# AdaLN layers on one core: setup cut to two modulation rows, step sizes finished per batch and stored in rows, half of the recurrence's first block loaded ahead

## The chip, the cores and the metric

The kernel runs on one core of a Trainium2 chip. The metric is the device time of one execution in microseconds (us); lower is better. All compute engines of the core take part: TensorE (PE in the profile, with PEld for its weight loads), VectorE (DVE), ScalarE (ACT), GpSimd (POOL). SyncE (SP) issues every DMA, from one queue.

## The reference

Two layers work on 16 batches of 512 tokens of 256 channels. Each layer has an attention part and a feed-forward part, each of them with a shift, a scale and a gate that come from a small conditioning vector per batch:

```python
mod = silu(c) @ wmod                       # per layer: 6 vectors of 256 for each batch
h = layernorm(x) * (1 + scale) + shift
# layer 0, attention part: a test-time-trained memory
q, k = l2norm(silu(short_conv(h @ W)));  v = silu(short_conv(h @ Wv))
lr = softplus(h @ Wlr.T + 0.001)           # two step sizes per token and head
# for each chunk of 16 tokens, one after the other:
k_h = softmax(k W_in) * lr[..., 1:];  q_h = softmax(q W_in)
o = q_h W_out + causal(q_h k_h) v
W_in, W_out = updated twice with lr of the chunk's first token
# then: o = layernorm(o) * gate @ Wo, a low-rank FFN, window attention, a gated FFN
```

The gates of both layers pass through a rule that keeps their size at 0.25 or more, with their sign.

## The kernel before, in words

Everything is one program, with semaphores set by hand: each engine has its own list of steps, and the order of the code is the order of execution. `Steps` names the values of a semaphore; `wait_ge(x.sem, x.at(n, "name"))` waits until that step of round n is done.

- **Setup.** SP loads the conditioning vectors and both layers' `wmod` (2 x 1.5 MB), three constants and 24 weights (`weights_loaded`). PE makes all 24 column blocks of the modulation (96 matmuls in the trace, L719) and the four gate rows (16, L725). ACT copies them out of PSUM, DVE adds one to the scales and makes the gates' sign and size in four dependent operations (L1749 to L1755). SP stores them in `gates_d`, and only behind this store, in the same queue, stands the first load of `x` (L488).
- **Phase A**, one iteration for each of 16 batches, on all engines at once. DVE: statistics of the next batch (L1762), for six tiles a convolution of three operations (L1785), and squares for the norms of q and k (L1794). ACT: `Ln` of the norms (L1223), the first step of the next layer norm (L1179, L1182), then for each tile the first tap of the convolution (L1201), between them `Exp` (L1187, L1227); then rows of k (L1236), `silu` of the tiles (L1211), gates (L1216), the raw step sizes (L1255) and the modulation of the next batch (L1194). PE: projections (L763), transposes (L736, L779), means of squares (L799). POOL: q and k times their inverse length (L1534). SP: stores of q and k (L492), the load of the next x but one (L488), `v_rows` and `k_rows` (L514), v, the gate, and the raw step sizes in `lr_d` (L514). `x` has one buffer (`a_x`).
- **`phase_a_done`**: every engine waits until all stores of phase A have landed, since the memory (`arena`) is used again with another layout.
- **Set-up of the recurrence.** SP loads the step sizes (L550, four DMAs in pieces of 64 bytes), twelve pieces of the first block of q, k, v (L557) and eight of the first chunk's rows (L565). ACT makes `Abs`, `Exp` and `Ln` of the 128 x 2048 step sizes, DVE adds the positive part (L1839) and copies every second one; PE picks rows (L820); POOL and DVE set areas to zero; POOL's last area, `kv`, stands in the memory in which the step sizes lie, so it waits for PE and DVE.
- **Recurrence** over 32 chunks, from PE's first sums (L846), then the other layers, two batches at a time, to the end.

The softplus is written as max(x, 0) + ln(1 + exp(-|x|)).

Of the kernel before, what the change touches and what calls it, by code (L numbers as in the profile page):

```python
# [6 lines left out]
P = 128  # L7
BATCH, TOK, DIM = 16, 512, 256
HEADS, HD = 16, 16
KT = DIM // P  # L10
# [62 lines left out]
def adaln_two_layers(nc, x, w_in, taps, w_out, ln_g, ln_b, w_in_init, w_out_init, u1, v1, b1, u2, v2, b2,  # L73
                     cond, wmod, w_attn, w_proj, w_r, w_k, w_v, mu, ident_c, blocks_c, parity_c, mask_c, four_c, scan_c, out):
    ctx = ExitStack()
    with ctx:
# [16 lines left out]
        lr_d = dram("lr_d", [CHUNKS, BATCH, CHUNK, 2 * HEADS])  # L93
# [43 lines left out]

        wmod_sb = carve(LAYERS, KT, N_MOD * DIM)
        cond_sb = carve(LAYERS, KT, BATCH)
        cond_silu = carve(LAYERS, KT, BATCH)  # L140
        g_raw = carve(2 * LAYERS * DIM)
        g_sign = carve(2 * LAYERS * DIM)
        g_size = carve(2 * LAYERS * DIM)
        gates_row = arena[0:BATCH, ARENA - 2 * LAYERS * DIM:ARENA]
# [18 lines left out]
        a_rows = [carve(TT, 2 * TOKROW) for _ in range(2)]  # L163

# [10 lines left out]
        kq_blk = [carve(TILES * 2 * BLOCK).rearrange("p (j g s t) -> p j g s t", j=JJ, g=GG, s=2) for _ in range(2)]  # L175
        v_blk = [carve(TILES * BLOCK).rearrange("p (j g t) -> p j g t", j=JJ, g=GG) for _ in range(2)]
        o_blk = [carve(TILES, BLOCK) for _ in range(2)]
        k_rows, v_rows = ([carve(TILES, ROW17) for _ in range(2)] for _ in range(2))
        kv = carve(JJ, PP * INNER * HD)
        run = carve(JJ, PP * INNER * HD)  # L180
# [15 lines left out]
        lr_raw, lr_tmp = (t.rearrange("p a b -> p (a b)") for t in (kv, run))  # L196
# [64 lines left out]
        su_act = Steps(sem("su_act"), ["silu", "modc", "raw0", "raw1"])  # L261
        su_pe = Steps(sem("su_pe"), ["mod", "gate0", "gate1"])
        su_dve = Steps(sem("su_dve"), ["identb", "plus1", "plus2", "plus3", "plus4", "tap", "side", "sign", "size", "gates"])
# [26 lines left out]
        st_pool = Steps(sem("st_pool"), ["no_o", "no_k", "ones_v", "no_rate", "one_q", "no_kv"])  # L290
        st_dve = Steps(sem("st_dve"), ["no_st", "no_q", "no_w", "in", "out", "lr", "tok", "row", "x0", "x1"])
        st_act = Steps(sem("st_act"), ["abs", "exp", "ln"])
# [127 lines left out]
        def phase_a_done(eng):  # L420
# [12 lines left out]
            eng.wait_ge(gates_stored, 16)  # L433
# [15 lines left out]
        def _(sp):  # L449

            sp.dma_start(cond_sb, cond.rearrange("l (k p) b -> p l k b", p=P)).then_inc(cond_loaded, 16)
            for layer in range(LAYERS):
                sp.dma_start(wmod_sb[:, layer], wmod[layer].rearrange("(k p) n -> p k n", p=P)).then_inc(wmod_loaded, 16)
            for dst, src in ((ident[:], ident_c), (mean16[:], blocks_c), (parity[:], parity_c)):
                sp.dma_start(dst, src).then_inc(consts_loaded, 16)
# [1784 lines left out]
```

## Time and profile before

| | |
|---|---|
| median of 3 runs | 2527.85 us (2524.26 to 2531.57) |
| the profiled execution: its time | 2533.14 us |
| its span, from the first instruction to the last | 2531.3 us |
| setup, to the first load of x | 0 to 43.3 us |
| phase A | 43.3 to 452.4 us |
| set-up of the recurrence | 452.4 to 477.6 us |
| busy: PE, DVE, ACT, POOL | 86%, 63%, 62%, 43% of the span |

The times in the rows are counted from the start of the span. An idle time in square brackets stands before the instruction, with the engine that ended it.

### The profile page before, as it was taken

How to read it: one execution, taken by the hardware profiler on the slowest of the kernel's cores; microseconds unless marked ns; L12 is line 12 of the kernel's file. 1: busy time of each engine (PE TensorE's matmuls, PEld its weight loads, DVE VectorE, ACT ScalarE, POOL GpSimd, SP SyncE). 2: the span in 40 equal slices, each digit the busy share in tenths (PEclk: the TensorE clock that was granted, in tenths of full speed). 3: DMA queues.
4: the chain of work that ended last, by engine and by line, in shares of the span. 5: the costliest groups of instructions: out<-in, count | busy, mean ns of one | idle time of the engine just before them, and what ended most of it. 6: DMA issues, size and time to landing. Idle time of an engine off the chain costs nothing.

```text
span 2531.3 us, 88431 instructions
## 1 busy us (share of the span) xinstructions
PE 2166.9 (86%) x32563; PEld 1390.6 (55%) x32563; DVE 1596.6 (63%) x3896; ACT 1576.2 (62%) x4079; POOL 1086.6 (43%) x1204
## 2 busy tenths in 40 slices
PE   5999997487788787787389999999999999999898
PEld 4554454255555555455246566575664756647466
DVE  1888886477666666667247477474764747647465
ACT  2788787377676666667248466484654846547464
POOL 0122122377677677667524423344233442334323
PEclk8999999699788888889699999999999999999999
DMA  4455555623233233231421231312213122130120
GB/s 150 126 158 164 162 156 160 119 68 85 66 79 74 68 85 76 56 72 39 137 52 31 71 75 43 94 32 66 67 48 94 42 58 60 52 89 4 39 50 18
DMA packets 403135, 201.57 MB, mean 80 GB/s; under 512 B 273776, under 2 KB 389104, under 8 KB 402688
## 3 DMA queue, kind: packets, MB, share of 16 engines
q1 hardware_dynamic: 402688, 195.65, 29.6%
q8 instruction: 276, 4.52, 0.8%
q14 instruction: 171, 1.40, 0.2%
HBM read 101.67 MB, written 69.27 MB: 68 GB/s over the span
## 4 chain that ended last, share of the span: by engine, by line
PE 55%; ACT 15%; issue 12%; DVE 12%; POOL 3%; DMA 1%; SPq 1%; ACTq 0%; DVEq 0%; POOLq 0%
PE psum L982 11%; PE psum L763 6%; ACT arena L1492 6%; ACT arena L1292 5%; PE psum L1075 4%; DVE arena L1785 4%; PE psum L834 3%; PE psum L846 3%; PE psum L1034 3%; PE psum L841 3%; PE psum L1042 3%; PE psum L1111 3%; PE psum L1148 2%; PE psum L1098 2%; PE psum L1129 2%
## 5 line engine op out<-in xcount | busy, mean ns | idle before, releaser
L1716 POOL TENSOR_TENSOR arena<-arena 128x400 f32<-128x400 f32 x256 | 218.3, 853 | 482.8 <-DVE arena L2132 482.8
L1292 ACT ACTIVATE arena<-psum,scan_sb 64x128 f32<-64x128 f32 x1152 | 308.3, 361 | 106.0 <-PE psum L911 88.4
L1492 ACT ACTIVATE arena<-psum,arena 128x100 f32<-128x100 f32 x1024 | 269.5, 365 | 6.0 <-DVE arena L2124 5.9
L1785 DVE SCALAR_TENSOR_TENSOR arena<-psum,taps_sb,arena 128x511 f32<-128x511 f32 (+2 forms) x288 | 213.8, 747 | 60.7 <-ACT arena L1201 53.9
L1534 POOL TENSOR_TENSOR arena<-arena 128x512 f32<-128x512 f32 x64 | 79.4, 1274 | 359.0 <-ACT arena L1227 359.0
L763 PE MATMUL psum<-arena,w_in_sb 128*128 128x512 f32 x512 | 230.0, 598 | 0.9 <-issue 0.9
L841 PE MATMUL psum<-arena 128*32 128x17 f32 x10240 | 134.9, 191 | 98.3 <-issue 65.1
L1852 DVE TENSOR_TENSOR arena<-psum,scan_sb 64x512 f32<-64x512 f32 x290 | 189.0, 673 | 7.6 <-PE psum L942 7.6
L846 PE MATMUL psum<-arena,scan_sb 128*128 128x512 f32 x264 | 186.5, 799 | 1.9 <-DVE arena L1852 1.9
L841 PEld LDWEIGHTS psum<-arena 128*32 128x32 f32 x10240 | 115.5, 117 | 123.1 <-issue 71.7
L2124 DVE TENSOR_REDUCE arena<-psum 128x4 f32<-128x400 f32 x256 | 146.4, 573 | 57.1 <-PE psum L1098 46.7
L1484 ACT ACTIVATE arena<-psum 100x512 f32<-100x512 f32 x256 | 155.7, 608 | 41.9 <-PE psum L1111 35.7
L1609 POOL TENSOR_TENSOR arena<-arena 128x512 f32<-128x512 f32 x128 | 133.6, 1065 | 93.5 <-ACT arena L1346 88.7
L1111 PE MATMUL psum<-ident,arena 128*100 128x128 f32 x1024 | 162.8, 282 | 4.5 <-ACT arena L1484 0.5
L2128 DVE TENSOR_REDUCE arena<-arena 128x4 f32<-128x400 f32 x256 | 145.6, 569 | 19.7 <-ACT arena L1492 13.6
L763 PEld LDWEIGHTS psum<-arena,w_in_sb 128*128 128x128 f32 x512 | 95.8, 192 | 110.6 <-issue 110.1
L1098 PE MATMUL psum<-arena 64*128 64x100 f32 x2048 | 156.1, 273 | 0.0
L834 PEld LDWEIGHTS psum<-arena 128*32 128x32 f32 x8192 | 89.2, 119 | 106.5 <-ACT arena L1292 77.1
L1558 POOL TENSOR_TENSOR arena<-arena 128x512 f32<-128x512 f32 x132 | 139.6, 1058 | 0.1
L1098 PEld LDWEIGHTS psum<-arena 64*128 64x128 f32 x2048 | 137.2, 190 | 0.0
L834 PE MATMUL psum<-arena 128*32 128x16 f32 (+1 forms) x8192 | 99.1, 195 | 30.1 <-issue 18.9
L1111 PEld LDWEIGHTS psum<-ident,arena 128*100 128x100 f32 x1024 | 102.9, 128 | 35.1 <-ACT arena L1484 12.9
(220 smaller groups left out, 4712.2 us busy)
## 6 DMA issues: line engine op xcount, KB each, us to landing
arena<-arena SPq DMA_DIRECT2D x144, 128.0 KB
arena<-x SPq DMA_DIRECT2D x32, 512.0 KB, 3.9
arena<-gates_d SPq DMA_DIRECT2D x112, 128.0 KB, 4.0
v_rows_d<-arena SPq DMA_DIRECT2D x64, 136.0 KB
k_rows_d<-arena SPq DMA_DIRECT2D x64, 136.0 KB
arena<-k_rows_d SPq DMA_DIRECT2D x128, 68.0 KB, 2.0
arena<-v_rows_d SPq DMA_DIRECT2D x128, 68.0 KB, 2.2
v_d<-arena SPq DMA_DIRECT2D x32, 256.0 KB, 4.3
```

The costliest lines, as they stand in the source:

```text
L763: mm = pe.matmul(bank[2 + j % 6][:], w_in_sb[:, k, j * P:(j + 1) * P], a_h[:, k], start=(k == 0), stop=(k == KT - 1))
L834: mm = pe.matmul(dst[j * NST:(j + 1) * NST, x], by_tile(st)[:, j, x], tok[:, j, x], start=True, stop=True)
L841: mm = pe.matmul(dst[j * NST:(j + 1) * NST, x], by_tile(pb)[:, j, x], rows[:, j * PP + x], start=True, stop=True)
L846: return pe.matmul(bank[RUN_BANKS[j]][:], causal, kv[:, j], start=True, stop=False, skip_group_check=True)
L982: mm = pe.matmul(B(s, banks[a])[:, j * DIM:(j + 1) * DIM], lhs(k, 2 * a + j), rhs(k), start=(k == 0), stop=(k == KT - 1))
L1098: mm = pe.matmul(B(s, top)[:, k * KEYS:(k + 1) * KEYS], c_qb[s][rows, k, f], c_k[s][rows, k, f], start=False, stop=True, skip_group_check= ...
L1111: mm = pe.transpose(bank[TURNED][0:KEYS, tok(u)], c_soft[s][:, f % 2, u], ident[:])
L1292: ins = act.activation(dst.rearrange("p (t x a) -> p t x a", x=PP, a=INNER)[upper, :, x], src.rearrange("p (t a) -> p t a", a=INNER)[upper ...
L1492: act.activation(c_soft[s][:, f % 2, u], sc, ACT.Exp, bias=c_max[s][:, u:u + 1]).then_inc(c_act.mark(f"exp{s}{f}u{u}"), 1)
L1716: pool.tensor_tensor(soft, soft, c_rec[s].unsqueeze(2).broadcast_to([P, 4, KEYS]), ALU.mult).then_inc(c_pool.mark(f"prob{s}{f}"), 1)
L1785: ins = dve.scalar_tensor_tensor(out=a_acc[:, t, j:TOK], in0=bank[2 + t][:, 0:TOK - j], scalar=taps_sb[:, t % KT, col:col + 1], in1=a_acc[ ...
L1852: return dve.tensor_tensor(dst.rearrange("p (t x a) -> p t x a", x=PP, a=INNER)[rows, :, xs], src.rearrange("p (t a) -> p t a", a=INNER)[r ...
```

## The change

- **Setup.** PE makes one row of 512 (shift and scale of the first layer's first part) from a first piece of `wmod` (512 KB), ACT copies it, four small transposes turn it, and that is all that batch 0 needs. `x(0)` is fifth in SP's queue; taps, `w_in` and `mean16` follow. The rest of `wmod` and 22 weights are issued behind x(1) and ahead of x(2). The other five rows of modulation, their copies, the gates and 20 transposes stand at the end of phase A.
- **Step sizes.** `rates(n)` on ACT (four operations on 128 x 128, between the last tap and the rows of k) and one sum on POOL finish them for each batch. `lr_d` is laid out as [batch, step, chunk, 32], and two DMAs with 4 KB runs load it ahead of `phase_a_done`. Each batch's store moves from the end of SP's iteration to a place ahead of the load of x.
- **One table.** At the head of each ACT sequence stands a load of the table that holds both `Ln` and `Exp`.
- **The first block.** Six of its twelve loads are issued ahead of the last batch's stores; the memory plan is moved so that they lie outside phase A's tiles.
- **Zeroing.** DVE's memset goes from 9216 to 4096 columns, POOL makes the other 5120; `kv` is set to zero at the start.

The diff, cut to its core:

```diff
-            sp.wait_ge(su_pe.sem, su_pe.before(1, "gate1"))
-            sp.wait_ge(su_dve.sem, su_dve.before(1, "gates"))
-            sp.dma_start(gates_d[0:BATCH], gates_row).then_inc(gates_stored, 16)
...
             load_x(0)
+            sp.dma_start(taps_sb[:], taps.rearrange("(k p) n -> p k n", p=P)).then_inc(taps_loaded, 16)
+            sp.dma_start(w_in_sb[:], w_in.rearrange("(k p) n -> p k n", p=P)).then_inc(w_in_loaded, 16)
+            sp.dma_start(mean16[:], blocks_c).then_inc(blocks_loaded, 16)
             next_x(1)
+            sp.dma_start(wmod_sb[:, 0, :, 2 * DIM:], wmod[0, :, 2 * DIM:].rearrange("(k p) n -> p k n", p=P)).then_inc(wmod_loaded, 16)
+            sp.dma_start(wmod_sb[:, 1], wmod[1].rearrange("(k p) n -> p k n", p=P)).then_inc(wmod_loaded, 16)
+            load_weights()
             next_x(2)
             store_rest(0)
             with sp.Fori(1, BATCH - 2) as n:
                 store_units(n - 1)
+                store_rates(n - 1)
                 next_x(n + 2)
-                store_rows_a(n - 1)
+                store_v_rows(n - 1)
+                store_k_rows(n - 1)
                 store_rest(n)
             for n in (BATCH - 2, BATCH - 1):
                 store_units(n - 1)
-                store_rows_a(n - 1)
+                store_rates(n - 1)
+                store_v_rows(n - 1)
+                store_k_rows(n - 1)
+                if n == BATCH - 1:
+                    for t in QKV:
+                        sp.wait_ge(a_stored[t], 16 * n)
+                    load_block(0, 0, range(JJ // 2))
                 store_rest(n)
+            store_v_rows(BATCH - 1)
             store_units(BATCH - 1)
-            store_rows_a(BATCH - 1)
+            store_rates(BATCH - 1)
+            store_k_rows(BATCH - 1)
+            sp.wait_ge(a_stored["lr"], 16 * TT * BATCH)
...
+            def mod_row(c):
+
+                layer, third = THIRDS[c]
+                for k in range(KT):
+                    mm = pe.matmul(bank[max(c + 1, 2)][0:BATCH], cond_silu[:, layer, k], wmod_sb[:, layer, k, third * 2 * DIM:(third + 1) * 2 * DIM],
+                                   start=(k == 0), stop=(k == KT - 1))
+                mm.then_inc(su_pe.mark(f"row{c}"), 1)
...
             turn_v(BATCH - 1)
+            pe.wait_ge(wmod_loaded, 16 * LAYERS)
+            pe.wait_ge(pr_act.sem, pr_act.at(BATCH - 1, "g1"))
+            for c in range(1, 6):
+                if c == 3:
+                    pe.wait_ge(le_act.sem, le_act.at(BATCH - 1, "ln3"))
+                mod_row(c)
             turn_k(BATCH - 1)
...
+            def rates(n):
+
+                act.wait_ge(pr_act.sem, pr_act.at(n, "lr"))
+                act.wait_ge(sp_pool.sem, sp_pool.before(n, "rate"))
+                act.activation(a_plus, a_lr, ACT.Relu).then_inc(sp_act.mark("plus"), 1)
+                act.activation(a_soft, a_lr, ACT.Abs).then_inc(sp_act.mark("abs"), 1)
+                act.wait_ge(sp_act.sem, sp_act.at(n, "abs"))
+                act.activation(a_soft, a_soft, ACT.Exp, scale=-1.0).then_inc(sp_act.mark("exp"), 1)
+                act.wait_ge(sp_act.sem, sp_act.at(n, "exp"))
+                act.activation(a_soft, a_soft, ACT.Ln, bias=1.0).then_inc(sp_act.mark("ln"), 1)
+
             def sequence(n, behind, ahead):
 
+                if behind or ahead:
+                    act.preload_act_table_set("natural_log_exp_and_others")
...
                 if behind:
+                    rates(n - 1)
                     rows_k(n - 1)
...
+            pool.memset(kv, 0.0).then_inc(st_pool.mark("no_kv"), 1)
             with pool.Fori(0, BATCH) as n:
                 units(n)
+                pool.wait_ge(sp_act.sem, sp_act.at(n, "ln"))
+                pool.wait_ge(a_stored["lr"], 16 * TT * n)
+                pool.tensor_tensor(a_rate, a_plus, a_soft, ALU.add).then_inc(sp_pool.mark("rate"), 1)
 
             phase_a_done(pool)
+            pool.memset(arena[:, 4 * TILES * NST:9 * TILES * NST], 0.0).then_inc(st_pool.mark("no_pb"), 1)
...
+            dve.wait_ge(lr_loaded, 16 * (JJ // 2))
+            for j in range(JJ):
+                ins = dve.tensor_copy(rate_tok[:, :, j * PP:(j + 1) * PP], rate_in[:, j // 2, j % 2].rearrange("q c (p i) -> q c p i", i=2)[:, :, :, 1])
+            ins.then_inc(st_dve.mark("tok"), 1)
             phase_a_done(dve)
-            dve.memset(arena[:, 0:9 * TILES * NST], 0.0).then_inc(st_dve.mark("no_st"), 1)
+            dve.memset(arena[:, 0:4 * TILES * NST], 0.0).then_inc(st_dve.mark("no_st"), 1)
```

SP's queue at the start, before: the last two weights, the store of the gates, then x (`arena<-x`).

```order
L482 DMA state<-w_in_init 128x128
L482 DMA state<-w_out_init 128x128
L485 DMA gates_d<-arena 16x1024 [waits su_dve,su_pe]
L488 DMA arena<-x 128x4x256
L488 DMA arena<-x 128x4x256 [waits ln_dve] x2
```

The same queue after the change, from its first DMA.

```order
L468 DMA arena<-cond 128x4x16
L469 DMA arena<-wmod 128x2x512
L471 DMA ident<-ident_c 128x128
L471 DMA parity<-parity_c 128x7
L474 DMA arena<-x 128x4x256
L559 DMA taps_sb<-taps 128x2x12
L560 DMA w_in_sb<-w_in 128x2x1056
L561 DMA mean<-blocks_c 128x128
L474 DMA arena<-x 128x4x256 [waits ln_dve]
L563 DMA arena<-wmod 128x2x1024
L564 DMA arena<-wmod 128x2x1536
L556 DMA w_out_sb<-w_out 128x2x256
```

The first x no longer stands behind 24 weights and the wait for the gates; 24 DMAs (two of wmod, 22 weights) now stand between x(1) and x(2).

ACT in the loop of phase A, before: from the first tap of the iteration (L1201) to the second.

```order
L1201 ACTIVATE arena<-psum,taps_sb 128x512 [waits pr_act]
L1185 ISA
L1186 ISA [waits ln_act]
L1187 ACT_TABLE_LOAD
L1187 ACTIVATE arena<-arena 128x4 [waits ln_dve]
L1226 ISA
L1227 ACTIVATE arena<-arena 128x512 [waits le_act]
L1198 REGISTER_ALU
L1199 REGISTER_ALU [waits pr_pe]
L1201 ACTIVATE arena<-psum,taps_sb 128x512 [waits pr_act]
```

The same place after the change (the tap is L1253 now).

```order
L1253 ACTIVATE arena<-psum,taps_sb 128x512 [waits pr_act]
L1237 ISA
L1238 ISA [waits ln_act]
L1239 ACTIVATE arena<-arena 128x4 [waits ln_dve]
L1278 ISA
L1279 ACTIVATE arena<-arena 128x512 [waits le_act]
L1250 REGISTER_ALU
L1251 REGISTER_ALU [waits pr_pe]
L1253 ACTIVATE arena<-psum,taps_sb 128x512 [waits pr_act]
```

And after the change from the last tap of the iteration to the table of `silu`: the four operations of `rates`, then the rows of k.

```order
L1253 ACTIVATE arena<-psum,taps_sb 128x512 [waits pr_act]
L1292 REGISTER_ALU
L1294 ACTIVATE arena<-arena 128x128 [waits sp_pool,pr_act]
L1295 ACTIVATE arena<-arena 128x128
L1297 ACTIVATE arena<-arena 128x128 [waits sp_act]
L1299 ACTIVATE arena<-arena 128x128 [waits sp_act]
L1283 REGISTER_ALU
L1288 ACTIVATE arena<-psum 128x4x8x16 [waits tr_pe,stored_krow]
L1288 ACTIVATE arena<-psum 128x4x8x16 [waits tr_pe]
L1257 ISA
L1263 ACT_TABLE_LOAD [waits le_pool]
```

One of the three table loads of an iteration is gone, and four small operations stand ahead of the rows of k.

SP's queue at the end of phase A after the change, from the last k_rows store of the batch before the last: six loads of q, k, v stand ahead of the last batch's stores.

```order
L498 DMA k_rows_d<-arena 8x16x272 x3
L522 DMA arena<-q_d 128x8x64 [waits stored_k1,stored_v0,stored_k0,stored_v1,stored_q1,stored_q0]
L522 DMA arena<-k_d 128x8x64
L522 DMA arena<-v_d 128x8x64
L522 DMA arena<-q_d 128x8x64
L522 DMA arena<-k_d 128x8x64
L522 DMA arena<-v_d 128x8x64
L478 DMA v_d<-arena 128x8x64 [waits pr_act] x2
L492 DMA gate_d<-arena 128x512 [waits pr_act] x2
L498 DMA v_rows_d<-arena 8x16x272 [waits tr_dve]
L498 DMA v_rows_d<-arena 8x16x272 x3
L478 DMA q_d<-arena 128x8x64 [waits le_pool] x2
```

Before, the k_rows stores of that batch were followed directly by the stores of v (`v_d`), the gate and the step sizes, then q, k, v_rows and k_rows of the last batch.

## Rows read from the trace of the kernel before

**Rows 1.** The chain that ended last, in order of time: start us, us, what

```profile
1.81 10.04 DMA arena<-wmod
11.89 20.66 PE psum L719 x96
...
43.33 3.69 DMA arena<-x
...
446.94 5.25 DMA k_rows_d<-arena
...
477.60 3.47 PE psum L846 x4
```

**Rows 2.** Timeline of the start: start us, us, engine, line, operation [idle before]

```profile
4.95 0.48 SPq L482 DMA_DIRECT2D w_out_sb<-w_out  x1
...
22.11 0.46 SPq L482 DMA_DIRECT2D state<-w_out_init  x1
...
50.79 0.20 ACT L1187 ACTIVATE arena<-arena 128x4 f32<-128x4 f32 x1
...
55.52 16.60 PE L763 MATMUL psum<-arena,w_in_sb 128*128 128x512 f32 x32 [0.91 <-issue]
...
77.42 1.40 DVE L1762 BATCH_NORM_STATS2 arena<-arena 128x6 f32<-128x256 f32 x4
```

**Rows 3.** Timeline of ScalarE in one iteration of phase A

```profile
286.77 0.27 ACT L1255 ACTIVATE arena<-psum 128x128 f32<-128x128 f32 x1
...
290.39 0.63 ACT L1211 ACTIVATE arena<-arena 128x512 f32<-128x512 f32 x1 [2.02 <-DVE arena L1785]
291.04 1.28 ACT L1223 ACT_TABLE_LOAD   x1
...
294.54 0.70 ACT L1201 ACTIVATE arena<-psum,taps_sb 128x512 f32<-128x512 f32 x1
295.26 1.28 ACT L1187 ACT_TABLE_LOAD   x1
...
302.83 0.69 ACT L1201 ACTIVATE arena<-psum,taps_sb 128x512 f32<-128x512 f32 x1 [1.03 <-PE psum L763]
...
305.80 2.19 ACT L1211 ACTIVATE arena<-arena 128x512 f32<-128x512 f32 x4
```

**Rows 4.** Timeline of VectorE in the same iteration

```profile
295.28 2.32 DVE L1785 SCALAR_TENSOR_TENSOR arena<-psum,taps_sb,arena 128x511 f32<-128x511 f32 x3 [3.07 <-ACT arena L1201]
297.89 2.32 DVE L1785 SCALAR_TENSOR_TENSOR arena<-psum,taps_sb,arena 128x511 f32<-128x511 f32 x3 [0.29 <-ACT arena L1201]
...
309.29 2.49 DVE L1794 TENSOR_TENSOR arena<-arena 128x512 f32<-128x512 f32 x4
...
313.92 1.40 DVE L1762 BATCH_NORM_STATS2 arena<-arena 128x6 f32<-128x256 f32 x4
```

**Rows 5.** Timeline of the DMA queue in the same iteration

```profile
307.39 0.40 SPq L488 DMA_DIRECT2D arena<-x  x1
```

**Rows 6.** One line's issues, 400 to 448 us: ns of an issue, min/median/max

```profile
L514 SPq DMA_DIRECT2D k_rows_d<-arena x12: 604/662/826, 400.1 to 446.9; - x12
```

**Rows 7.** The block loads' line, 452 to 480 us: the same columns

```profile
L557 SPq DMA_DIRECT2D arena<-k_d x4: 584/1128/1148, 462.3 to 472.0; - x4
```

**Rows 8.** Timeline of phase A's end and of the recurrence's set-up

```profile
423.40 2.91 SPq L514 DMA_DIRECT2D k_rows_d<-arena  x4
...
444.76 2.83 SPq L514 DMA_DIRECT2D k_rows_d<-arena  x4
...
452.50 1.45 POOL L1541 MEMSET arena<- 128x512 f32 x3 [10.78 <-DMA k_rows_d<-arena]
...
454.46 7.74 DVE L1833 MEMSET arena<- 128x9216 f32 x1 [20.81 <-issue]
...
455.02 0.95 POOL L1548 MEMSET w_in_sb<- 128x1024 f32 x1
...
475.36 1.80 POOL L1551 MEMSET arena<- 128x2048 f32 x1 [19.39 <-PE psum L820]
```

More of the change, by code:

```diff
@@ L140, in adaln_two_layers @@
         cond_silu = carve(LAYERS, KT, BATCH)
[L141 to L144, printed above, removed]
+        first_rows = carve(2 * DIM)[0:BATCH]
+        gates_row = carve(2 * LAYERS * DIM)[0:BATCH]
+        THIRDS = [(layer, third) for layer in range(LAYERS) for third in range(N_MOD // 2)]
         top[0] = 0
@@ L260, in adaln_two_layers @@
         weights_loaded = sem("weights_loaded")
-        su_act = Steps(sem("su_act"), ["silu", "modc", "raw0", "raw1"])
-        su_pe = Steps(sem("su_pe"), ["mod", "gate0", "gate1"])
-        su_dve = Steps(sem("su_dve"), ["identb", "plus1", "plus2", "plus3", "plus4", "tap", "side", "sign", "size", "gates"])
+        wmod_first, taps_loaded, w_in_loaded, blocks_loaded = sem("wmod_first"), sem("taps_loaded"), sem("w_in_loaded"), sem("blocks_loaded")
+        su_act = Steps(sem("su_act"), ["silu", "row0", "modc0"])
+        su_pe = Steps(sem("su_pe"), ["row0", "mod0"] + [f"row{c}" for c in range(1, 6)] + ["mod1"])
+        su_dve = Steps(sem("su_dve"), ["tap", "plus1"] + [f"row{c}" for c in range(1, 6)]
+                       + ["side", "sign", "size", "gates", "modc1", "plus2", "plus3", "plus4", "identb"])
         x_loaded = sem("x_loaded")
@@ L289, in adaln_two_layers @@
         st_pe = Steps(sem("st_pe"), ["rates", "turn"])
[L290 to L292 removed]
+        st_pool = Steps(sem("st_pool"), ["no_kv", "no_pb", "no_o", "no_k", "ones_v", "no_rate", "one_q"])
+        st_dve = Steps(sem("st_dve"), ["tok", "no_st", "no_q", "no_w", "in", "out", "row", "x0", "x1"])
+        sp_act = Steps(sem("sp_act"), ["plus", "abs", "exp", "ln"])
+        sp_pool = Steps(sem("sp_pool"), ["rate"])
         re_dve = Steps(sem("re_dve"), [
@@ new lines, in _ @@
+            load_weights()
+            next_x(2)
+            store_rest(0)
+            with sp.Fori(1, BATCH - 2) as n:
+                store_units(n - 1)
+                store_rates(n - 1)
+                next_x(n + 2)
+                store_v_rows(n - 1)
+                store_k_rows(n - 1)
+                store_rest(n)
+            for n in (BATCH - 2, BATCH - 1):
+                store_units(n - 1)
+                store_rates(n - 1)
[5 more added lines that the diff above has]
+                    load_block(0, 0, range(JJ // 2))
+                store_rest(n)
@@ L752, in project @@
                     elif name in ("q0", "q1"):
-                        pe.wait_ge(pr_act.sem, pr_act.before(n, ("g0", "g1")[j]))
+                        if behind:
+                            pe.wait_ge(pr_act.sem, pr_act.before(n, ("g0", "g1")[j]))
                     elif behind:
```

262 lines of the change are left out of this document (132 added, 130 removed).

## The prediction

> **What bounds the kernel now.** I read the chain of work that ended last first. Its long pieces ahead of the loops tell where the change can reach [rows 1]: the load of all of `wmod` (10.04 us), PE's 96 modulation matmuls (20.66 us), the load of x that starts only at 43.33, and at the other end the last k_rows store, whose landing takes 5.25 us and closes phase A at 452.19; PE's first sums of the recurrence start at 477.60. So 43.3 us pass before x is asked for, and 25.4 us between the end of phase A and the recurrence. Nothing behind 477.60 is touched by the diff but addresses; I take it as unchanged, with 3 us either way for gaps of no visible cause.
>
> Then one iteration of phase A, engine by engine. ACT ends the last `silu` at 291.02 and starts the table load at 291.04; then `Ln`, then the first tap at 294.54 to 295.24 [rows 3]. DVE starts its convolution when that tap is there (295.28, idle 3.07) and works without a gap until 313.92 and on, except 0.29 us before the second tile (297.89) [rows 4]. DVE's last convolution releases the last `silu` of ACT, which had waited 2.02 us for it [rows 3]. That loop, DVE to ACT and back, sets the period, 23.65 us (statistics at 77.42 and, ten iterations later, at 313.92 [rows 2, 4]): ACT counts from the last `silu` to the first tap, DVE for the rest. ACT's time between the taps and the last `silu` has slack.
>
> **The start.** x(0) is the fifth DMA. Before, the eighth stood at 4.95 [rows 2], so x goes out at about 3. The first piece of `wmod` and x are each 512 KB; such a load took 3.69 us alone, and 3.1 MB took 10.04 us, 0.31 MB per us [rows 1]. So `wmod`'s piece lands at about 5.5 and x at about 7. PE's row is four recorded matmuls of 512 columns: 0.52 us each as in the mean of the first projections [rows 2], 0.87 as in the recurrence's first sums [rows 1], so 2.1 to 3.5 us; I take 2.1. ACT's copy of 512 columns is priced at 0.6 (a 512-column `silu`: 0.63 [rows 3]), four transposes, the small copy and the addition together at 1.5, an estimate from operations of 0.27 [rows 3]. Modulation is ready at 9.7. The statistics of x take 1.40 [rows 2] and some 0.4 more and are ready by 9.3. Behind that stand what stood there before: a table load (1.28), `Ln`, a table load (1.28 [rows 3]), `Exp`: `Exp` starts at about 13.0. From `Exp` to the first projection it was 50.79 to 55.52 [rows 2], 4.7 us, so the projection starts at 17.8 instead of 55.52. Rounded for small gaps, **37.5 us less**. Bounds: if all 2.3 MB of the first eight DMAs land together (9.2) and PE's row takes 3.5, it is 33; with none of the small gaps 39.
>
> What is late next is x(2): it stands behind 24 DMAs. Their issue costs about what 22 weights cost before, 4.95 to 22.57, 17.6 us [rows 2], plus 1 for two more: from 15 to 33.6. The data, 7 MB at 0.31 MB per us, is through at 37.6, and x(2) lands at about 39. The statistics that need it started at 77.42 [rows 2], now 39.9. It is just in time, and DVE has 3.07 us of idle time behind these statistics [rows 4], so up to 3 us of lateness cost nothing.
>
> **The loop.** Removed from ACT: the table load at 295.26, 1.28 us [rows 3]. It lies between first and second tap; DVE waits only 0.29 of it [rows 4], so 0.27 us per iteration is gained, in 15 iterations **4.0 us less**. The other load, at 291.04, only changes its table. Added to ACT: four operations on 128 columns, 0.27 each [rows 3], 1.1 us, behind the last tap (ends 303.52). They delay the four `silu` from 305.80 to 306.9; the first ends at 307.5 and DVE needs it at 309.29 [rows 3, 4]: hidden, and the 2.02 us ahead of the last `silu` hide the rest. If they took 0.6 each (2.4 us), the last `silu` would be late by 0.4 and the gain gone. SP's step-size store now stands ahead of x and waits for POOL's sum, which is ready at about 303.5 + 1.1 + 0.4 = 305.0; four issues at 0.66 [rows 6] and gaps end at 307.8 to 308.4. x went out at 307.39 [rows 5]; it goes out up to 1.1 us later and lands at 312.1 instead of 311.1, needed at 313.92 [rows 4]. Nothing lost. v_rows and k_rows behind it are stored later by as much and get it back, since the store is no longer behind the gate.
>
> ScalarE's price of a switch is where the Trainium skill and the rows part. The row has the next operation right behind the load: 1.28 us is all of it [rows 3]. "ScalarE: Activation LUTs", section "What ACT_TABLE_LOAD costs", adds a drain of about 1.38 us to the 1.28 for every switch. By the row the loop gives 4.0; by the page a load taken away would be worth 2.66 on ACT, yet no more than the 0.29 that DVE waits there, unless the drain hid in the stretch ahead of the tap.
>
> **The end of phase A.** SP becomes the late one here. Before, it ended batch 14's k_rows at 426.31 and its last issue at 447.59 [rows 8], 21.3 us for 20 DMAs at 0.66 and a gap, 13.6 us, and waits. Now: the sum of the step sizes of batch 14 is ready five periods of 23.65 behind 305.0, at 423.3; four step-size stores, four v_rows, four k_rows, about 8.2 us with gaps: 431.5. Six block loads at 1.13 [rows 7] and gaps: 438.4. Then the same 20 DMAs, now all ready: 452.0. That is **4.3 us later** than 447.59, and the landing behind it (5.25) puts the end of phase A at 456.6. It covers what was added elsewhere: PE's 20 recorded matmuls for the other five rows, 8.7 to 10.4 us ahead of the transposes of k, must only be through before SP comes to k_rows, at 449, where it came at 444.76; ACT's 1.1 us and DVE's gate work lie under the same cover. Without it PE's rows would cost their part beyond SP's old time.
>
> **Set-up of the recurrence.** Gone from the path: four loads of step sizes in small pieces ahead of the blocks, three ACT operations over 2048 columns, DVE's sum, six block issues of 1.13 and the `kv` memset (1.80 [rows 8]). Left on POOL: 5120 columns at 1.80/2048, 4.5 us, and its old memsets, 452.50 to 455.97, 3.5 us [rows 8]: from 456.7 to 464.7. Left on DVE: the step sizes land at 456 to 458.5 (issued at 452; 512 KB took 3.69 [rows 1], behind k_rows), four copies of 256 columns, about 1; 4096 columns of zeros at 7.74/9216, 3.4 [rows 8]; small copies and two spreads, about 3: 464 to 466. I take 465.0 for the first sums instead of 477.60: **12.6 us less**, the 4.3 included. SP's blocks are issued by 464 and needed at 468.5, behind the sums (3.47 [rows 1]); rows of k and v later.
>
> Splitting the zeroing needs POOL and DVE at once. The row shows them so: DVE's memset runs 454.46 to 462.20, and POOL's 1024 columns inside it take 0.95, per column what its 2048 take (1.80) [rows 8]. The Trainium skill, "SBUF — State Buffer", section "SBUF: two separate sides", has a shared port pair as an exclusive lock between GpSimd and a VectorE operation in a two-port mode; the trace shows none for memsets.
>
> **Sum.** -37.5 - 4.0 - 12.6 = -54.1. Against the profiled execution's own 2533.14 that is 2479.0; it lay 5.3 above the median of the runs, so **2474 us** for the median.
>
> **Rivals.**
> - *SP is not late at the end*: block loads are issued faster (0.58 was the shortest [rows 7]) or the stores' waits are shorter. The 4.3 go: 2470. For it: 7.7 of its 21.3 us were waits. Against: the count above. Then PE's rows come into view.
> - *The start gives less*: PE's row at the longer duration, loads that land together, x(2) late by more than 3 us. At -31: 2480. For it: a weight load with tiny pieces holds SP, and 24 DMAs in front of x(2) leave no slack.
> - *The loop gives nothing*, because the added operations eat it: 2478.
> - *The zeroing excludes itself*: POOL's 4.5 us behind DVE's 3.4, first sums 3.4 later: 2477. Against: the row inside DVE's memset. [...]
> - *Slower than before*: x comes late in every iteration, since it waits for ACT's four operations, POOL and four issues. Its place is DVE's statistics at 313.92. The period grows once x lands later than now by more than 2.8 (311.1 to 313.92) and about 2 of DVE's 3.07 idle us (the rest ACT needs for `Ln` and the tap), 4.9 in all; to eat 54 us in 14 iterations it must be 3.9 more, 8.8, so an issue at 316.2 where I expect 308.4. At 317 it would be 0.8 x 14 = 11 us slower than before, 2539. No row speaks for it.
> - *The change doesn't do what it says*: if a table load came back in the loop, 1.28 us stay between the taps: 2478, as with the loop giving nothing.
>
> **Chances.** Forecast 0.62; SP not late 0.11; start less 0.15; loop nothing, 0.06; zeroing 0.03; slower 0.02; other small ones 0.01. Least and most of the terms: -39 - 5 - 17 gives 2467, -33 + 0 - 8 gives 2487; with 3 us for the rest below and 1 above (a bound of every term at once is unlikely) the range is 2464 to 2488. About 0.3%, 8 us, is what a measurement of this kernel can tell from none: faster 0.975, same 0.005, slower 0.02.
>
> **What would show it.** Right: first projection at about 18; statistics of x(2) without a long DMA wait; a period of 23.4; the second tile's wait gone; SP without a wait from batch 14's k_rows to the last k_rows issue, some 20.5 us; POOL's long memset 4 to 5 us behind the landing; first sums some 8.3 us behind the end of phase A. Wrong: a first projection past 22, a period above 23.65, a DMA named as releaser of the statistics in the loop, or chunks of the recurrence that take longer than before.

## The result: 0.6% slower, where 2.1% faster was forecast

The changed kernel takes 2545.84 us (median of 7 runs, 2536.06 to 2548.93), the kernel before 2527.85 (7 runs): a ratio of 1.0058, 95% interval 1.0035 to 1.0081. The forecast was 2474, range 2464 to 2488. The profiled execution took 2548.93, its span is 2547.1 where it was 2531.3.

The chain that ended last, after the change, at the places of [rows 1] and [rows 8]: start us, us, what.

```profile
1.26 4.16 DMA arena<-wmod
5.55 3.59 PE psum L757 x4
...
18.59 12.83 PE psum L808 x24
...
413.75 6.20 DMA arena<-lr_d
...
421.41 1.90 DVE w_in_sb L1910 x3
424.11 3.47 DVE arena L1913
...
430.25 3.75 PE psum L899 x4
```

Up to the first sums (L899 is the old L846) the change did nearly what was forecast: the first projection starts at 18.59 and not at 55.52, the first sums at 430.25 and not at 477.60, 47.4 us earlier. From there to the end of the span the kernel before takes 2531.3 - 477.60 = 2053.7 us and this one 2547.1 - 430.25 = 2116.9. So 63.2 us were lost in code that the diff doesn't touch. Nearly all of them lie in the recurrence: 60.4 in the stretch from the first to the last of its 32 chunks (by ACT's copy, L1326 and L1388). That stretch before, as windows give it: stretch, us, busy us and count of PE, PEld, DVE, ACT, POOL, granted clock, DMA share, GB/s.

```profile
481.89:1187.99 706.10, 559.75 (x19540) 374.50 (x19532) 472.89 (x1395) 473.92 (x1584) 494.86 (x586) 0.87 0.31 71
```

And after.

```profile
435.16:1201.69 766.53, 592.82 (x19547) 393.00 (x19541) 476.68 (x1395) 476.49 (x1584) 498.39 (x589) 0.81 0.29 65
```

The work is the same: the counts of DVE and ACT are equal, those of PE and POOL within 10. PE is busy 33.1 us longer at a granted clock of 0.81 in place of 0.87, and idle 27.4 us longer; DVE, ACT and POOL are busy for as long as before, within 1%. So it is PE. What it waits for in this stretch, after the change: line, what ended the wait, us in total, times, longest.

```profile
PE psum L887 <- issue: 51.4, 32, 3.0
...
PE psum L894 <- issue: 37.2, 34, 2.2
...
PE psum L907 <- issue: 5.3, 4, 1.8
```

"issue" says that the profile shows nothing that was waited for. The same rows of before give 82.0 us in 59 waits, these with two smaller ones 98.3 in 76. Single waits show more. PE's timeline after the change, in a run of three groups of 64 update matmuls:

```profile
1006.65 0.74 PE L894 MATMUL psum<-arena 128*32 128x17 f32 x64
1007.59 0.73 PE L894 MATMUL psum<-arena 128*32 128x17 f32 x64 [0.20 <-DVE arena L1925]
1008.50 0.67 PE L894 MATMUL psum<-arena 128*32 128x17 f32 x57 [0.18 <-ACT arena L1353]
1011.13 0.25 PE L894 MATMUL psum<-arena 128*32 128x17 f32 x7 [1.96 <-issue]
...
1013.91 1.26 PE L887 MATMUL psum<-arena 128*32 128x16 f32 x108 [0.50 <-DVE arena L1925]
1017.40 0.51 PE L887 MATMUL psum<-arena 128*32 128x16 f32 x20 [2.23 <-issue]
```

PE stops in the middle of a group, 57 matmuls in, with nothing to wait for, and again 123 matmuls later. One round of the loop earlier it stops behind the same 57 (811.52), one later too (1209.83). Before the change the same groups run like this:

```profile
1008.09 0.68 PE L841 MATMUL psum<-arena 128*32 128x17 f32 x59 [0.18 <-DVE arena L1852]
1011.24 0.94 PE L841 MATMUL psum<-arena 128*32 128x17 f32 x69 [2.46 <-issue]
```

One stop, 62 matmuls earlier in the code. A recorded f32 matmul is two instructions, a weight load and a matmul. The stops can be placed by counting all of PE's records in the trace, register and branch instructions included, with the turns of the loops taken out. Between the first and the last chunk PE has 38 waits of more than 1.2 us before the change and 49 after. Three of each stand at the loop's first matmuls. All the others lie behind an instruction whose number in the program is 201 to 203 over a multiple of 256 (to within the few instructions that the trace doesn't record), 35 before and 46 after. The recurrence loop has 10,375 instructions on PE. It starts at instruction 801 before, 33 over a multiple of 256, and at 675 after, 163 over one: the diff took 126 instructions of modulation, waits and set-up from PE's code ahead of it.

### The profile page after: what moved, and what is told of

The parts are those of the page before. It is cut to its first block, busy times and chain, and to the rows that moved or that the text cites. A ratio compares the mean times of both kernels' runs of the same rounds, so it can differ in the third digit from the quotient of the medians.

```text
span 2547.1 us, 88423 instructions
## 1 busy us (share of the span) xinstructions
PE 2187.3 (86%) x32499; PEld 1393.0 (55%) x32499; DVE 1596.5 (63%) x3901; ACT 1565.8 (61%) x4121; POOL 1102.3 (43%) x1221
## 4 chain that ended last, share of the span: by engine, by line
PE 48%; DVE 16%; issue 15%; ACT 15%; POOL 2%; SPq 2%; DMA 1%; DVEq 1%; ACTq 1%; POOLq 0%
PE psum L1035 11%; ACT arena L1554 8%; DVE arena L1846 6%; PE psum L1128 4%; PE psum L899 4%; PE psum L887 3%; PE psum L894 3%; PE psum L1087 3%; PE psum L1095 3%; ACT arena L1353 3%; PE psum L907 2%; PE psum L1201 2%; PE psum L1067 2%; PE psum L1164 2%; DVE arena L1855 1%
## 5 line engine op out<-in xcount | busy, mean ns | idle before, releaser
L1353 ACT ACTIVATE arena<-psum,scan_sb 64x128 f32<-64x128 f32 x1152 | 311.5, 362 | 122.4 <-PE psum L964 60.4
L899 PE MATMUL psum<-arena,scan_sb 128*128 128x512 f32 x264 | 194.7, 829 | 3.8 <-issue 2.0
L894 PE MATMUL psum<-arena 128*32 128x17 f32 x10240 | 140.3, 196 | 64.5 <-issue 39.6
L894 PEld LDWEIGHTS psum<-arena 128*32 128x32 f32 x10240 | 122.0, 124 | 90.2 <-issue 49.1
L887 PEld LDWEIGHTS psum<-arena 128*32 128x32 f32 x8192 | 93.9, 122 | 137.5 <-ACT arena L1353 74.6
L887 PE MATMUL psum<-arena 128*32 128x16 f32 (+1 forms) x8192 | 105.5, 198 | 59.5 <-issue 52.6
```

Of the source, the lines that this page charges most:

```text
L887: mm = pe.matmul(dst[j * NST:(j + 1) * NST, x], by_tile(st)[:, j, x], tok[:, j, x], start=True, stop=True)
L894: mm = pe.matmul(dst[j * NST:(j + 1) * NST, x], by_tile(pb)[:, j, x], rows[:, j * PP + x], start=True, stop=True)
L899: return pe.matmul(bank[RUN_BANKS[j]][:], causal, kv[:, j], start=True, stop=False, skip_group_check=True)
L1353: ins = act.activation(dst.rearrange("p (t x a) -> p t x a", x=PP, a=INNER)[upper, :, x], src.rearrange("p (t a) -> p t a", a=INNER)[upper ...
```

## The experiments

**Theory:** PE's instructions come in blocks of 256. Where PE runs through a block faster than the next one comes, it stands still, and where the loop stands against these blocks (below: its place, the number of its first instruction over a multiple of 256) decides how often. **Rivals:** the moved memory plan (blocks, `kv` and `run` at other addresses); the clock by itself, since the recurrence starts 47 us earlier; the place of the code of ACT, DVE or POOL.

### Moving PE's loop, and nothing else

```diff
+            for _ in range(126):
+                hold(pe)
             pe.wait_ge(weights_loaded, 16 * 22)
             pe.wait_ge(lr_loaded, 16 * (JJ // 2))
```

`hold` is an increment of a semaphore that nobody waits for. PE idles there. In `b_pe130` 130 of them stand ahead of the kernel before's `phase_a_done(pe)`.

a_pe126: 

> The kernel after, with 126 semaphore increments more on PE, which does nothing else at that place: behind the setup's last product and ahead of its wait for the step sizes (PE idles there from 401 to 420 us). No work, address, order or wait is another; only PE's recurrence loop stands again where it stood in the kernel before, counted from the program's start (instruction 801 in place of 675). Theory, placement of PE's code: the loop loses the 62 us that it gained; the recurrence takes 753 to 760 us in place of 817.8 and the whole 2480 to 2492. Rival, memory layout of the loop's operands: nothing changes, 2546. Rival, the clock gate through the 47 us earlier start: 2546. Rival, placement of the code of ACT, DVE or POOL: 2546.

b_pe130: 

> The kernel before, with 130 semaphore increments more on PE where it waits for the end of phase A, so that its recurrence loop stands as in the kernel after (instruction 931, which is 675 and 256 more). Theory, placement of PE's code, with a period of 256 instructions: the recurrence takes 812 to 822 us in place of 755.4 and the whole about 2590. If the placement matters but the period is another, some other value. Rivals, layout, clock through the start time, code of the other engines: 2528.

Measured: `a_pe126` 2486.61 us (4 runs), ratio to the kernel before 0.9815, interval 0.976 to 0.9869. It takes 700.6 us from the first to the last chunk. `b_pe130` 2597.34 (5 runs), ratio 1.0237, interval 1.0186 to 1.0288, and 755.1 us. The kernel before took 2538.54 in the same rounds, on another chip than in the result above. So the place alone adds 2.4%, 59 us, to the kernel before. Taken from the changed kernel it is worth as much, by the ratios (1.0058 over 0.9815) 2.5%, some 60 us. In `a_pe126` the groups shown above break where they did before the change:

```profile
959.65 0.68 PE L896 MATMUL psum<-arena 128*32 128x17 f32 x59 [0.19 <-DVE arena L1927]
963.09 1.26 PE L896 MATMUL psum<-arena 128*32 128x17 f32 x69 [2.75 <-issue]
```

All three rivals fall: `a_pe126` has the new memory plan, the early start (first sums at 429.91) and the other engines' new code. `b_pe130` stands 256 instructions behind the changed kernel and is slow like it, though not to the microsecond (755.1 and 766.5 us in the stretch), so the period is 256 or a part of it. It isn't half of it: the places 33 and 163 lie 130 apart and differ by some 60 us. In both runs the waits of more than 1.2 us, but for three at the loop's start, are again at 201 to 203 over a multiple of 256, 35 in `a_pe126` and 41 in `b_pe130`.

The expectations that speak of 755 and 818 us count from the first sums to the end of PE's last transposes of outputs (L914, L861 before), some 50 us more than this stretch. Counted so, `a_pe126` took 748.7 and `b_pe130` 806.4, both about 5 us under their ranges.

### The time as a function of the place

The same edit with other counts.

a_pe64: 

> The kernel after with 64 such increments on PE at the same place: the loop starts at instruction 739. Theory, placement: the recurrence takes another time than both 755 and 818 us, most likely between (some 790, the whole some 2517), and PE's waits at fixed places of the loop sit 64 instructions earlier in it. Rivals: 818 and 2546, the waits at the same places.

a_pe192: 

> The kernel after with 192 such increments on PE at the same place: the loop starts at instruction 867. Theory, placement: some value of its own, most likely between 755 and 818 us in the recurrence (some 785, the whole some 2512), with PE's waits 192 instructions earlier in the loop than in the kernel after. Rivals: 818 and 2546.

a_pe94: 

> The kernel after with 94 increments on PE ahead of the recurrence: the loop starts at instruction 769, one behind a multiple of 256. Theory, blocks of 256 instructions: PE's waits without a releaser lie again where the instruction's number in the program is about 198 and a multiple of 256, so 32 instructions later in the loop than with the loop at 801; counting the blocks that PE runs through faster than 3.9 us (median of the runs so far) gives about as many as there: 700 to 725 us from the first to the last chunk (706 and 701 at 801, 720 at 867, 743 at 739, 767 and 755 at 675 and 931), whole 2480 to 2505. Rival, what the 126 increments restored was something else than the place modulo 256: no order in the numbers.

a_pe158: 

> The same with 158 increments: the loop starts at instruction 833, 65 behind a multiple of 256, between the two best places so far (33 and 99). Theory, blocks of 256: 700 to 722 us from the first to the last chunk, whole 2480 to 2502, PE's waits 32 instructions earlier in the loop than with 801. Rival as before.

a_pe158t: 

> The kernel after with 158 increments on PE once more (loop at 833, 65 behind a multiple of 256), timed in rounds, since the one look gave 2474. Theory: the place 65 is better than 33 by what the look showed, 8 to 9 us in the recurrence (692.4 to 700.6 us from the first to the last chunk): 2470 to 2485, ratio to the kernel before 0.975 to 0.981. Rival, the two places are alike and the look was the low end of the scatter: 2482 to 2492.

a_pe142: 

> The kernel after with 142 increments: the loop at instruction 817, 49 behind a multiple of 256, halfway between 33 and 65. Theory, the time depends on the place smoothly, since a boundary moves by 16 of a group's 256 instructions and more: 692 to 705 us from the first to the last chunk, the whole 2472 to 2486. Rival, it jumps at single places: anything up to 2520.

a_pe174: 

> The kernel after with 174 increments: the loop at instruction 849, 81 behind a multiple of 256, halfway between 65 and 99. Theory, smooth: 692 to 721 us from the first to the last chunk. The last loop, behind the recurrence, took 1340.6 us with 192 increments and 1322 to 1326 with all others; theory, it has a bad place of its own (its first instruction 184 behind a multiple of 256 there, 166 here): 1324 to 1341 here, whole 2475 to 2520. Rival, the 16 us behind the recurrence were scatter: 1324.

| loop's first instruction, over a multiple of 256 | first to last chunk, us | granted clock there | whole, us |
|---|---|---|---|
| 1 (a_pe94) | 729.3 | 0.82 | 2509.16 |
| 33 (before; a_pe126) | 706.1; 700.6 | 0.87; 0.86 | 2527.85; 2486.61 |
| 49 (a_pe142) | 692.5 | 0.86 | 2473.55 |
| 65 (a_pe158; a_pe158t) | 692.4; 689.6 | 0.87; 0.88 | 2474.07; 2474.23 (5 runs) |
| 81 (a_pe174) | 696.2 | 0.85 | 2478.39 |
| 99 (a_pe192) | 720.4 | 0.82 | 2521.06 |
| 163 (after; b_pe130) | 766.5; 755.1 | 0.81; 0.84 | 2545.84; 2597.34 |
| 227 (a_pe64) | 743.0 | 0.81 | 2521.95 |

The whole times come from several chips, on which the kernel before took 2527.85 to 2538.54, and those of places 1, 49, 81, 99, 227 and of `a_pe158` are single executions. The stretch itself scatters: in the runs further down it is 702.8 and 706.9 us at place 33 and 696.9 to 699.2 at 65. So there is one valley from 33 to 81, inside which the places can't be put in order by this table, and one hill near 163. The place 65 is some 70 us better than the one that the change happened to give.

In the expectations' own count, place 227 took 790.5 us where 790 was guessed, and 99 took 768.7 where it was 785. The place 1 lies above its range (729.3 for 700 to 725) and 65 below its own (692.4 for 700 to 722): the count of fast blocks that gave the former was no good guide. Behind the recurrence, place 81 took 1323.2 us, below the 1324 to 1341 of the theory and next to the 1324 of its rival, so a bad place of the last loop isn't shown there. Where `a_pe192` took 16 us more was not tested; in its last layers PE's waits without a releaser on L1078 are 11.7 us in 12, in `a_pe174` 2.0 in 4. `a_pe158t` has a ratio of 0.9789 to the kernel before, interval 0.9764 to 0.9814.

b_pe32: 

> The kernel before with 32 increments on PE where it idles ahead of the recurrence, so that its loop starts at instruction 833, 65 behind a multiple of 256, as in the best kernels. Theory, the place alone decides: the recurrence takes 690 to 695 us from the first to the last chunk in place of 706.1, the whole is 11 to 16 us lower, ratio 0.994 to 0.996. Rival, the gain of the place 65 belongs to the changed kernel with its other memory plan: 706 and 1.000.

Measured: 2524.77 (12 runs), ratio 0.9948, interval 0.993 to 0.9966; 698.5 us from chunk to chunk, where 690 to 695 were expected. The place works in the kernel before as well, by the ratio as forecast; of the 13 us that it says, 7.6 are seen in this stretch of the profiled execution.

### The loop of phase A: one part alone

```diff
             def sequence(n, behind, ahead):

+                if behind or ahead:
+                    act.preload_act_table_set("natural_log_exp_and_others")
```

b_tab: 

> The kernel before with one part of the change alone: the load of the table with both Ln and Exp at the head of each sequence on ACT. PE's loop stands where it stood. Theory, the whole gain of the loop comes from the table load between the first and the second tap: the period falls from 23.65 to 23.27 as in the kernel after, DVE's first two tiles run as six operations without a gap in 4.54 us, and 15 x 0.38 = 5.7 us go from phase A; 2520 to 2524 where the kernel before takes 2527. Rival, 0.27 comes from it and the rest from the step sizes' store that left SP's iteration: period 23.38, 4 us. Rival, nothing: 23.65.

Measured: statistics of the ten iterations start at 76.35 and 309.00, a period of 23.27, to the digit that of the changed kernel; first sums at 471.04, 6.6 earlier. Median 2531.7 (10 runs) against 2535.66 on that chip, ratio 0.9989, interval 0.9972 to 1.0006: too small for the runs to tell, plain in the trace. Row of DVE behind the first tap, in `b_tab`:

```profile
314.01 4.54 DVE L1787 SCALAR_TENSOR_TENSOR arena<-psum,taps_sb,arena 128x511 f32<-128x511 f32 x6 [3.08 <-ACT arena L1201]
```

Two tiles in 4.54 where [rows 4] has 2.32, 0.29 of waiting and 2.32: 4.93 from start to end. So all 0.38 us come from the one table load.

### The first block's loads put back

```diff
-                if n == BATCH - 1:
-                    for t in QKV:
-                        sp.wait_ge(a_stored[t], 16 * n)
-                    load_block(0, 0, range(JJ // 2))
...
-            load_block(0, 0, range(JJ // 2, JJ))
+            load_block(0, 0, range(JJ))
```

In the two split kernels the 158 increments stand in three places:

```diff
+            for _ in range(30):      # PE's start
+                hold(pe)
...
+            for _ in range(30):
+                hold(pe)
             pe.wait_ge(su_act.sem, su_act.at(0, "modc0"))
...
+            for _ in range(98):
+                hold(pe)
             pe.wait_ge(weights_loaded, 16 * 22)
```

a_noblk (with 126 increments): 

> The kernel after with the loop at 801 (126 increments) and the six early block loads put back behind the end of phase A, in front of the other six. Theory, SP's queue binds the end of phase A: the last issue of the k_rows stores comes 7.2 us earlier (406 in place of 413.2), and the step sizes land and DVE starts as much earlier; twelve loads of 1.13 us behind the end of phase A then last until about 427 and the last lands at about 430, so PE waits some 3 us for them behind its first sums: the whole some 4 us faster than with the six ahead (2486.6), 2481 to 2485. Rival, the block loads become the bound: first products of the block later than now, 2488 to 2494. Rival, something else than SP ends phase A: no change at its end, and the six issues come on top, 2490 to 2494.

a_noblk158: 

> The same place (158 increments) and the six early block loads behind the end of phase A. With the loop at 801 this put the first sums 6.1 us earlier (423.7 in place of 429.9) and the span 3.8 lower, while the medians were alike. Theory, it gives 2 to 4 us here too: 2468 to 2482. Rival, nothing: as the kernel with 158 increments alone. Rival, a loss in the first block: 2 to 5 us more than that.

a_split: 

> The kernel after with the loop at 833 as before, but of the 158 increments 30 stand at PE's very start, 30 ahead of its first transposes and 98 ahead of the wait for the step sizes, all in stretches in which PE idles. One increment took 0.147 us (158 in 23.2). Theory, nothing in the early kernel hung on the 158 with the block loads ahead: first sums at 429.8 as before, 2470 to 2478. Rival, the increments at the start delay the first projection: 2 to 5 us more.

a_split_noblk: 

> The same with the six block loads behind the end of phase A. With 158 increments in one place DVE waited 4.68 us for PE's product of the step sizes and the first sums came at 428.4 and not at 423.7. Theory: that wait goes, first sums at 423.5 to 424.5, first chunk at 429, and the whole is 4 to 5 us below the kernel with the loads ahead: 2466 to 2472. Rival, the last block load, which lands at 427.5, holds PE's first products up, and the gain stays under 2 us.

Measured: `a_noblk` 2487.45 (5 runs; 2481 to 2485 expected; ratio 0.9804, where `a_pe126` has 0.9815: no difference to be told, though its first sums start at 423.73 and not at 429.91), `a_noblk158` 2472.65 (6 runs; 0.9776, interval 0.9748 to 0.9805; on that chip `a_pe158t` took 2474.23), `a_split` 2479.14 (5 runs; 0.9772, interval 0.9751 to 0.9793), `a_split_noblk` 2472.24 (5 runs; 0.9753, interval 0.9728 to 0.9779). The last two, on one chip with the same increments, differ by 6.9 us where 4 to 5 were expected, but their intervals overlap; their first sums start at 432.75 and 425.48, 3 us and 1 us later than expected. With the loads behind and the loop at 65 the kernel is 2.2 to 2.5% faster than the kernel before, the best measured. In `a_noblk158` the increments themselves, 0.147 us each, held DVE up in the set-up:

```profile
426.15 0.69 DVE L1917 COPY arena<-psum 128x512 f32<-128x512 f32 x1 [4.68 <-PE psum L869]
```

Without the early loads SP issues the step sizes' load at 406.62 (`a_noblk`) instead of 413.25, and the rest follows; the block loads, all twelve behind the end of phase A, land at 427.5 and delay PE's first product of the block by less than a microsecond. So loading ahead, one of the change's aims, puts the first sums 6 to 7 us later, because the queue that it lengthens is the one that ends phase A. That the whole gets longer by it isn't shown: the three pairs differ by about 3 (by the ratios), 1.6 and 6.9 us, each within its noise. The 30 increments at the very start of `a_split` delayed the modulation row from 5.55 to 7.09, as its rival had it.

## Why the prediction was wrong

**The step that failed** is the last sentence of its first paragraph: "Nothing behind 477.60 is touched by the diff but addresses; I take it as unchanged, with 3 us either way". The diff touches one thing more: how many instructions stand ahead of PE's loop. The term that the sum put at nothing was worth +63 us at the changed kernel's place. With the loop put back to 33 the rest of the mechanism stands: `a_pe126` has a ratio of 0.9815, 46.8 us of 2527.85 (by its interval 33 to 61), where the sum was -54.1 and the terms ahead of the recurrence came to -47.4. The waits were to be seen in the trace of before, as 82 us of "issue" on PE's two fastest lines; the prediction allowed 3 us for such gaps and did not ask what they hang on.

**The start** (-37.5): -36.9. PE's row took 3.57 us, the long end, where 2.1 was taken, so the modulation was ready at 10.75 and not at 9.7; x's statistics, begun at 7.74, were ready before it, at 9.67. x(2) was 1.56 us late for DVE, within the 3 us allowed:

```profile
41.80 1.41 DVE L1823 BATCH_NORM_STATS2 arena<-arena 128x6 f32<-128x256 f32 x4 [1.56 <-DMA arena<-x]
```

**The loop** (-4.0): -5.7. The period is 23.27. Only the size was off: I took 0.27 of the wait of 0.29, and 0.38 came, since six operations run on without a stop take 4.54 us and two times three with the wait between them 4.93.

ACT around the period's turn, after, at the places of [rows 3]:

```profile
262.71 0.30 ACT L1294 ACTIVATE arena<-arena 128x128 f32<-128x128 f32 x1
...
263.80 1.07 ACT L1288 ACTIVATE arena<-psum 128x512 f32<-128x512 f32 x2
264.88 1.28 ACT L1263 ACT_TABLE_LOAD   x1
266.18 2.19 ACT L1263 ACTIVATE arena<-arena 128x512 f32<-128x512 f32 x4
...
272.95 0.63 ACT L1263 ACTIVATE arena<-arena 128x512 f32<-128x512 f32 x1 [1.59 <-DVE arena L1846]
```

The four added operations are hidden as forecast: the last `silu` still waits 1.59 us for DVE. The table load starts 0.01 us behind the rows of k and the next operation 0.02 us behind the load. The Trainium skill, "ScalarE: Activation LUTs", section "What ACT_TABLE_LOAD costs", adds a drain of about 1.38 us to the 1.28 us of the load; this trace shows none.

**End of phase A** (+4.3): +8.2. SP's last k_rows issue ends at 413.20; 447.59 less 36.9 and 5.7 would be 405.0. From batch 14's k_rows to there it was 24.6 us where 20.5 were forecast. The six loads took 7.2 of them, near their 6.8. The term that was too small is the 20 stores: 17.1 us where 13.6 were counted at 0.66 each; two issues of k_d alone took 3.08. `a_noblk`, in which the last k_rows issue ends at 406.57, takes 6.6 of the 8.2 back.

```profile
388.83 0.46 SPq L522 DMA_DIRECT2D arena<-q_d  x1
...
396.12 2.35 SPq L478 DMA_DIRECT2D v_d<-arena  x2
...
404.19 3.08 SPq L478 DMA_DIRECT2D k_d<-arena  x2
...
410.66 2.54 SPq L498 DMA_DIRECT2D k_rows_d<-arena  x4
```

**Set-up** (12.6 less, the 4.3 included): 4.8 less. From the last k_rows issue to the first sums it is 17.1 us and not 13.0. The step sizes land 6.20 us behind their issue, and DVE's four copies took 3.34 us in place of 1:

```profile
419.98 3.34 DVE L1910 COPY w_in_sb<-arena 128x256 f32<-128x256 f32 x4 [15.65 <-DMA arena<-lr_d]
424.11 3.47 DVE L1913 MEMSET arena<- 128x4096 f32 x1 [0.80 <-issue]
```

POOL in the same place:

```profile
416.98 4.37 POOL L1606 MEMSET arena<- 128x5120 f32 x1 [18.95 <-DMA k_rows_d<-arena]
421.28 1.89 POOL L1608 MEMSET arena<- 128x512 f32 x3
...
424.38 0.95 POOL L1615 MEMSET w_in_sb<- 128x1024 f32 x1
```

POOL, at whose 464.7 I had both engines meet, was done 5 us before the first sums, and its 5120 columns took 4.37. While DVE's memset ran, POOL's 1024 columns took 0.95 as in [rows 8]: memsets don't exclude one another. DVE's copies and POOL's memsets seem to. The first copy, begun at 419.98, ends at 421.49, 0.15 us behind POOL's long memset (421.34), and each of the other three ends 0.14 to 0.15 behind one of POOL's three short ones. It is so for the four copies in every run of the changed kernel, wherever the first begins; it takes 0.78 to 2.33 us, the later ones 0.69 (one 0.37). Before the change the copies had DVE and the memory to themselves, with POOL idle:

```profile
473.24 0.90 DVE L1843 COPY w_in_sb<-arena 128x256 f32<-128x256 f32 x4
```

So the price of 1 us was right for copies alone, and the change put them beside POOL's zeroing, which made them 2.4 us longer, on the path to the first sums. POOL pays too: its three memsets of 512 columns take 1.89 us beside the copies, 1.45 in [rows 8]. No run was made to part the two, so that they hold each other up rests on these ends and durations. It accounts for over half of the 4.1 us that set-up missed; the rest lies in the step sizes' landing (6.75 us behind the last k_rows issue, where 4 to 6.5 were forecast) and in gaps around DVE's work.

So the terms ahead of the recurrence make -47.4 where -54.1 was forecast, and what lies behind the first sums +63.2. Of the rivals "SP not late" fell, "start less" did too (0.6 us less, where it meant 6.5), and the kernel was slower on a path that no rival named. The prediction's last line had the right sign to look for: "chunks of the recurrence that take longer than before".

**What stays open.** Of the 60.4 us between the chunks' stretches, 16.3 are waits without a releaser. 33.1 are PE being busy longer at a lower mean granted clock (0.81 for 0.87), more of it at 1.2 GHz and less at 2.4. The remaining 11 are nearly all other waits of PE, for ACT, DVE and POOL; that they follow from the first two is argued, not shown. In the table the clock mostly goes down as the stretch grows longer, but no run separated the two; whether the waits pull the clock down stays open.

## What to carry to other kernels

Before you trust "this part is untouched", count the instructions that the change adds or removes ahead of each fast loop, and look for "issue" waits that split a group of small matmuls at the same count in every round of the loop. If they are there, scan the loop's place with a few dozen idle instructions in steps of 16 to 32 over one period before you judge any change: here the scan is worth more than the change (70 us against 47). And a load moved ahead is only free if its queue isn't the one that ends the phase: here it put the first sums 6 to 7 us later.

## What the runs showed of the hardware

PE's code comes through a queue of its own. From the page of the changed kernel, part 3: queue, kind, packets, MB, share.

```profile
q8 instruction: 273, 4.47, 0.7%
```

That is 16.4 KB a packet, and 64,998 recorded matmuls and weight loads come to 238 a packet, beside register and semaphore instructions. Taken one by one from the trace, these packets answer the open "issue" waits. In the timeline of PE above, packets end at 1009.87 and 1016.11, and PE goes on at 1011.13 and 1017.40, 1.3 us behind each. Before the change one ends at 1009.92, and PE goes on at 1011.24. It is so for all 49 waits of more than 1.2 us between the first and the last chunk after the change, and for all 38 before: each ends 1.2 to 2.1 us behind the end of such a packet. The number of packets in that stretch is nearly the same, 164 and 161; four rounds of the loop, 41,500 instructions, are 162 blocks of 256. So it isn't more code that is brought, but more of it comes too late.

A run of 128 small matmuls, 256 instructions, takes 1.3 to 2.0 us where it isn't broken (1.66 and 1.84 in single rows of before and after), and the packets in the recurrence start 4.2 us apart before and 4.5 after, by the median. Such a run is through before the next block is there. One example with other work in the block: 123 records that end at 1015.17, 4.0 us behind 1011.13, are followed by the next only at 1017.40.

The Trainium skill, "Runtime: NRT & Kernel Launch", section "Instruction fetch mechanics", has the blocks as they are seen here, 16 KiB or 256 instructions. It also says that the fetch is mostly hidden, since instructions are issued more slowly than they are brought. The trace disagrees: waits of 1.2 to 3.0 us, all but three at the loop's start 201 to 203 instructions over a multiple of 256, and some 70 us between the best and the worst place.

DVE's copies from memory to memory and POOL's memsets took turns in all 13 runs of the changed kernel, as shown above: 52 copies, each ending 0.14 to 0.15 us behind one of POOL's memsets, while DVE's own memset ran beside POOL's without a loss on either side (3.47 us for 4096 columns, 7.74 for 9216 before). The rows name no wait for this: the copies just take longer.
